# Centring two quads of each group on GpSimd instead of VectorE in a graph-LSTM kernel

## The reference

```
h = relu(layernorm(x))
h = relu(adj @ (h @ Wg0 + bg0)) ; h = relu(adj @ (h @ Wg1 + bg1))
for p in 1..4:                       # skip lengths
    last = LSTM over windows of p positions of h (zero start), last hidden state
    h[:, window ends] = last
x = x + h
h = relu(layernorm(x))
out[t] = x[t] + adj[t,t]*(h[t]@W0) + sum_{s>t} adj[t,s]*(h[s]@W1) + sum_{s<t} adj[t,s]*(h[s]@W2) + bias
```

## Time and profile before

| what | value |
|---|---|
| median of 3 runs | 416.67 us (416.29 to 416.74) |
| the profiled execution itself | 416.46 us |
| its span from the first to the last instruction | 414.5 us |
| granted TensorE clock | 1.000 of full speed |
| busy: PE, VectorE, ScalarE, GpSimd | 399.9, 338.2, 288.1, 40.8 us |

### The profile page before, as it was taken

One profiled execution on the slowest core, in us unless ns is written; L12 is line 12 of the kernel. 1 busy time (PEld: TensorE's weight loads), 2 busy tenths in 40 slices (PEclk: granted clock), 3 DMA queues, 4 the chain that ended last, 5 costly groups with the idle time before them and its releaser, 6 DMA issues. The chain is left out here.

```text
span 414.5 us, 6535 instructions
## 1 busy us (share of the span) xinstructions
PE 399.9 (96%) x2401; PEld 347.9 (84%) x2401; DVE 338.2 (82%) x858; ACT 288.1 (70%) x579; POOL 40.8 (10%) x43
## 2 busy tenths in 40 slices
PE   8999999999999999999989999999998999999987
PEld 7787889897987889799867879899786788989765
DVE  5568989897988789787987788978996867787884
ACT  4767766675897777676687676767587677776544
POOL 4910002000300002000110000200110000000220
DMA  7820000000000000000000000000000000000012
GB/s 233 317 86 2 0 0 2 0 2 2 0 1 27 1 27 0 27 2 1 2 0 25 27 0 27 1 27 2 0 2 26 25 2 25 2 26 2 1 51 78
DMA packets 5215, 11.18 MB, mean 27 GB/s; under 512 B 1088, under 2 KB 2112, under 8 KB 4672
## 3 DMA queue, kind: packets, MB, share of 16 engines
q1 hardware_dynamic: 5184, 10.77, 7.2%
HBM read 6.57 MB, written 4.19 MB: 26 GB/s over the span
## 5 line engine op out<-in xcount | busy, mean ns | idle before, releaser
L825 ACT ACTIVATE GT<-PS,BG 128x256 f32<-128x256 f32 (+2 forms) x312 | 158.1, 563 | 17.7 <-PE PS L524 12.2
L496 PE MATMUL PS<-HH,WIH 128*128 128x256 f32 (+2 forms) x312 | 107.6, 345 | 2.6 <-DVE HH L973 1.9
L497 PE MATMUL PS<-HH,WIL 128*128 128x256 f32 (+2 forms) x312 | 102.7, 330 | 0.0
L505 PE MATMUL PS<-HL,WIH 128*128 128x256 f32 (+2 forms) x294 | 97.4, 331 | 0.1
L831 ACT ACTIVATE TC<-CS 128x512 f32<-128x512 f32 (+2 forms) x88 | 45.2, 513 | 50.5 <-DVE CS L949 38.2
L496 PEld LDWEIGHTS PS<-HH,WIH 128*128 128x128 f32 x312 | 58.8, 188 | 10.8 <-DVE HH L980 2.9
L364 POOL TENSOR_TENSOR RS<-VE,NHALF 128x4 f32<-128x4 f32 (+2 forms) x17 | 29.2, 1718 | 362.6 <-DVE VE L897 362.6
L497 PEld LDWEIGHTS PS<-HH,WIL 128*128 128x128 f32 x312 | 58.9, 189 | 4.1 <-issue 1.2
L505 PEld LDWEIGHTS PS<-HL,WIH 128*128 128x128 f32 x294 | 55.5, 189 | 6.1 <-DVE HL L988 2.0
L524 PE MATMUL PS<-SL,WHH 128*128 128x256 f32 (+2 forms) x192 | 60.0, 313 | 0.0
L520 PE MATMUL PS<-SH,WHH 128*128 128x256 f32 (+2 forms) x192 | 59.8, 312 | 0.0
(11 more groups left out here) (96 smaller groups left out, 655.0 us busy)
## 6 DMA issues: line engine op xcount, KB each, us to landing
out_tbd<-X SPq DMA_DIRECT2D x15, 256.0 KB, 2.0
X<-x_tbd SPq DMA_DIRECT2D x3, 1024.0 KB, 13.1
X<-x_tbd SPq DMA_DIRECT2D x4, 256.0 KB, 4.2
WI<-wih_t SPq DMA_DIRECT2D x1, 1024.0 KB, 5.8
WH<-whh_t SPq DMA_DIRECT2D x1, 768.0 KB, 7.3
out_tbd<-X SPq DMA_DIRECT2D x2, 128.0 KB, 1.7
WL<-w_l SPq DMA_DIRECT2D x1, 192.0 KB, 6.6
WG<-wg SPq DMA_DIRECT2D x2, 64.0 KB, 3.4
```

The lines of the kernel that those rows point to most:

```text
L496: pe.matmul(dst, WIH[:, p - 1, cols], x_high, start=True, stop=False)
L497: pe.matmul(dst, WIL[:, p - 1, cols], x_high, start=False, stop=False)
L505: mm = pe.matmul(dst, WIH[:, p - 1, cols], x_low, start=False, stop=(j == 0))
L825: act.activation(GT[:, s, q, 0:n], bank(s, q)[:, 0:n], ACT.Tanh if q == C else ACT.Sigmoid, bias=BG[:, 4 * (p - 1) + q:4 * (p - 1) + q + 1 ...
```

## The change

GpSimd centres quads 2 and 3 of groups 0 to 2. In its queue the two instructions stand behind `group(i)`. CENTRE 2 waits for the last gate activation of unit 4 of the next pass, CENTRE 3 for that of unit 7 (`GATES_BEFORE[5]` and `GATES_BEFORE[8]` count the gates in front of units 5 and 8); CENTRE 2 also waits for the means and for TensorE's last turn of the group before, which read the same tile H3. VectorE's two instructions for these quads go, with their places at units 5 and 10. The semaphore `centred` and its counts stay. The last group is centred on VectorE as before.

```diff
-START_LATE = {4: ((OWN, 0),), 5: ((CENTRE, 2),), 10: ((CENTRE, 3),)}
+START_LATE = {4: ((OWN, 0),)}
+CENTRE_AT = {2: 5, 3: 8}
...
+            def centre(i, q):
+
+                if q == ON_SCALAR:
+                    pool.wait_ge(var2, 2 * STREAMS * i + 4)
+                    pool.wait_ge(turn_mm, QUADS * i)
+                pool.wait_ge(gate_act, GATES * (i + 1) + GATES_BEFORE[CENTRE_AT[q]])
+                part = slice(i * G + q * PACK, i * G + (q + 1) * PACK)
+                pool.tensor_tensor(H3[:, quad(q), :], X[:, part, :],
+                                   MINUS2[:, quad(q)].unsqueeze(2).broadcast_to([T, PACK, D]),
+                                   ALU.add).then_inc(centred, 1)
+
             for i in range(GROUPS - 1):
                 group(i)
+                for q in range(ON_SCALAR, QUADS):
+                    centre(i, q)
...
             def centre(g, q):
 
-                if g == GROUPS - 1:
-                    wait_apart(dve, var2, 2 * STREAMS * g + 2 * q + 2, x_quarter[0], 16)
-                elif q % 2 == 0:
-                    wait_apart(dve, var2, 2 * STREAMS * g + q + 2, x_quarter[0], 16)
+                wait_apart(dve, var2, 2 * STREAMS * g + 2 * q + 2, x_quarter[0], 16)
```

More of the change, by code:

```diff
@@ L86 @@
 FILL = {4: 6, 9: 6, 15: 5}
-LOW, OWN, ADD, CENTRE = "low", "own", "add", "centre"
+LOW, OWN, ADD = "low", "own", "add"
 LAST = QUADS - 1
@@ L1092, in last_step @@
                     return
-                if what == CENTRE:
-                    centre(g, q)
-                elif what == LOW:
+                if what == LOW:
                     turn_down(g, q, home(plan, TURN, q))
```

## The result

The changed kernel takes 418.42 us (median of 5 runs, 418.19 to 418.49), the kernel before 416.51 us (5 runs). The ratio is 1.0045, 95% interval 1.003 to 1.0059: slower, as forecast, by 1.9 us and not by 3.9. The profiled execution took 418.49 us, 2.0 us more than that of before.

A forecast was written before the change was run, and what follows sets the result against it. TensorE was taken to bound the kernel, VectorE mattering only where TensorE waits for it. The profiled 416.46 us plus 3.63 for CENTRE 3 and 0.3 for CENTRE 2 gave 420.4 us, range 416.3 to 421.8.

The forecast's parts named there:

- I take 1.21 us: Cost of one centring to VectorE, priced by the weight split on GpSimd, within bounds of 0 and 1.27 us.
- CENTRE 3's term: Between unit 7's cell and LOW 2, VectorE loses 1.21 us in each of three passes: 3.63 us.
- Where TensorE stops: At VALUE 8, waiting for LOW 2; idle time there grows from 0.2 to 1.4 us, three times.
- CENTRE 2's term: Unit 4's hidden state 0.44 us late; 0.3 us lost in all, in the first pass; idle time takes the others.
- The freed slots are worth nothing: Six instructions leaving VectorE, 4.1 us of busy time, gain nothing, as VectorE idles for gates behind both slots.
- Who wins a tie: At 241.93 GpSimd or L949 goes first; either way VectorE loses about 1.2 us before LOW 2.
- Not slower: Rival: GpSimd's reads don't stop VectorE, or GpSimd is held back until LOW 2; 416.5 us, chance 0.18.
- Shared: Rival: both engines run, VectorE at about half speed while they overlap; 418.5 us, chance 0.08.
- A slower add: Rival: the broadcast operand makes GpSimd's add take 1.8 us; up to 423.4 us, chance 0.08.
- Faster: Rival: VectorE's freed slots count after all, 0.5 us in each of three passes; 415.0 us, chance 0.04.

The follow-up runs named there:

- the kernel with OWN 1 out of the way: Changed kernel with OWN 1 moved one unit earlier on VectorE, behind unit 6's low part: 416.45 us, ratio 1.0005 to the kernel before.
- the halved add: Changed kernel with CENTRE 3 covering only two of its four batches (128x256): 416.9 us, ratio 1.0016 to the kernel before.
- the kernel with idle starts: Changed kernel with GpSimd's adds started when unit 5's and unit 6's low parts are written: 416.21 us, ratio 0.9996 to the kernel before.
- the faster order: Kernel before with LOW 2 and three ADDs moved earlier, centring on GpSimd in VectorE's idle times: 410.72 us, ratio 0.9866.

## Why the prediction was wrong, and where it held

The direction, the run of VectorE that is hit and the mechanism were right; the size was not, nor the matmul at which TensorE stops. The step that failed is "I take 1.21 us" for what one centring costs VectorE, and with it the term 3 x 1.21 = 3.63 us. The runs showed 0.78 us of waiting in its place, and 0.65 of them reached TensorE.

- **CENTRE 3's term.** Measured 0.65 us a pass at unit 9, 2.0 us in all. Three things make the difference of 0.5 us a pass. The add is shorter than the split: 1.04 us. VectorE isn't kept out for all of it: OWN 1 could start at 243.38 and lasted 0.78 us too long, so it got its operands at about 243.38 + 0.78 = 244.16, while GpSimd's row ends at 242.78 + 1.58 = 244.36; the last 0.2 us of the row don't block, and 0.06 us of the add's 1.04 had gone by when OWN 1 started (243.38 - 242.78 = 0.60, of which GpSimd waited 0.54). And 0.1 us was covered: from OWN 1's start to the hidden state's it is 1.46 us instead of 0.78, which is 0.68 more and not 0.78, because the hidden state has to wait for tanh as well, as the kernel with OWN 1 out of the way shows. I took the whole duration for the hold (the time for which VectorE is kept out), although my own bounds said 0 to 1.27 and no row showed where in an instruction the port is let go. In the halved add the hold was 0.35 us.
- **Where TensorE stops.** I had it wait for LOW 2 at VALUE 8, with its idle time there growing from 0.2 to 1.4 us. That didn't come: 0.22 us, as before. The hidden state of unit 7 is late too, and unit 9's matmuls read it before VALUE 8 comes up. For the sum it makes no difference, as both are late by the same time; but a kernel with LOW 2 moved ahead would still pay at unit 9 (argued, not run).
- **CENTRE 2's term.** I said 0.44 us late and 0.3 us lost in the first pass. It was 0.22 late and 0.16 lost (gate F), by the same error in the hold: the add ran from 126.96 to 128.00, and the hidden state, from 127.64, got its operands 0.22 later at about 127.86. That the idle time takes it in the other two passes held: TensorE falls back by nothing there.
- **The freed slots are worth nothing.** Held to within the interval of 0.5 us, by the kernel with idle starts, and again in the faster order.
- **Who wins a tie.** I left this open between L949, L1044 and L976, and that didn't matter: the instruction behind the tie paid.
- **Rivals.** Not slower: refuted, by the rows of OWN 1 and by the time; but its time is what one gets by moving either side. Shared (418.5 us): the time fits it by luck, the rows don't: L963 kept its 0.69 us while GpSimd waited 0.54, and CENTRE 2 kept its 1.04 us while the hidden state waited 0.22. One engine waits each time, and the other isn't slowed. A slower add: refuted (1.04 us). Faster: refuted.

By the Trainium skill, page "SBUF — State Buffer", section "SBUF: two separate sides", the shared pair is an exclusive lock: whichever instruction starts first gets it for the whole instruction, and the other fully blocks. The trace agrees that the second waits, in both directions (GpSimd 0.54 us, OWN 1 0.78). It differs on the length as the profile's rows have it, 0.78 us of a 1.04 us add, and the measurement decides.

The range from 416.3 to 421.8 us held the time. Its centre was 2 us off, because I worked with the upper end of a cost whose bounds were 0 and 1.27 us, instead of asking how much of an instruction's row is its start and end. VectorE's own rows show that kind of thing: L1055 starts at 243.38, 0.09 us before the row of L963 ends (242.78 + 0.69), and L990 at 244.84, 0.07 us before that of L1055 does.

What stays open: why the weight split takes 1.27 us where the add takes 1.04, and which part of GpSimd's row, at its start or its end, doesn't keep VectorE out.

## What to carry to other kernels

Work moved to GpSimd is not free because GpSimd is idle: its SBUF operands keep VectorE's two-SBUF-input instructions out, here for 0.78 us for a 1.04 us add of 128x512. Start it with the event that makes VectorE idle, not with one that makes VectorE busy; here that alone was worth the 2 us. And count what leaves an engine only where a faster engine is waited for: 4.1 us off VectorE gave nothing, while four of its steps moved ahead of TensorE's stops gave 5.7.

## What the runs showed of the hardware

- GpSimd's add of 128x512 takes 1.04 us unhindered, with a broadcast or a full operand, rounded or plain result, add or subtract. Behind a VectorE instruction that started with it, 1.58; with 256 elements 1.16. So a further 256 elements take 0.42 us, and VectorE was kept out for 0.35 us by 256 and 0.78 by 512.
- The wait shows as a longer VectorE instruction, with no idle time and no releaser. The view of waits for 243 to 250 us has no line for it (TensorE's are put down to L994 and L1047, behind it); an instruction's duration against that of its like (1.53 against 0.75) shows it.
